# Who issues the stores of the scan-input stage: SyncE's queue or GpSimd's

## The chip, the cores and the metric

The kernel runs on one core of a Trainium2 chip. The metric is device time in microseconds (us) of one execution. TensorE (PE) multiplies matrices, VectorE (DVE) and ScalarE (ACT) work element by element, GpSimd (POOL) does so too, and SyncE (SP) here only issues DMAs. POOL can issue DMAs as well. An engine carries out its own instructions in the order in which they are written; semaphores order the engines among each other.

## The reference, cut to what matters

The program is a chain of four image networks; each is cut into stages that hand tensors over through memory. The change lies in the first stage of the last network, which prepares a selective scan:

```
xn = layernorm over the channels of x3, times ln_w, plus ln_b
xc, z = split(in_proj_w @ xn)                        # 192 channels each
xc = silu(depthwise 3x3 convolution(xc) + conv_b)
dts, B, C = split(x_proj_w @ xc)                     # 12 + 4 + 4 rows for each of 4 directions
z is needed later only as silu(z)
```

The stage writes `xc`, `zs` (silu of z), `dts` and `bcs` (B and C, each number split into three bf16 parts).

## The kernel before

`scan_inputs` works on 14 chunks, s = 0 to 13. A chunk is 8 image rows (448 columns) of two images together: 384 channels, laid as three tiles of 128 partitions. Each engine's program is one loop over s = 0 to 18 (`LAST`), and each loop step holds work of several chunks:

- PE in step s: `centre(s)` (the mean is taken off, from `xin`, line 2907 and the following, into `pA`), `project(s-1, 0)` (into `pI`, the half that becomes xc), `moment(s)` (the mean square, again line 2907 and the following), `small(s-4)` (lines 2951 to 2960: dts and B, C), `project(s-1, 1)` (the gate half).
- ACT in step s: `square(s)` (copies the centred chunk and squares it, lines 2985 and 2986), `maps(s-1)` and `halo(s-1)` (the convolution's input), `root(s)` (logarithm L3009 and exponential L3011), `small(s-4)`, `middle(s-4)`, a table load, `gates(s-1)` (silu of z into `zo`, L3031), `inputs(s-3)` (silu of the convolution into `xo`, L3037), a table load.
- DVE in step s: `taps(s-3, 0, 6)`, `normal(s)` (L3107, the normalised chunk `xn`), `remainder(s-4)`, `taps(s-3, 6, 9)`, `low(s-4)`. A tap is three instructions.
- SP in step s: the load of `xin` for chunk s (L2862; four buffers, so it needs `centred` of chunk s-4, `centred >= s-3`), then the store of `zo` of chunk s-1 (L2866), then for chunk s-4 the stores of `xo` (L2871), of `do` (two, L2874) and of `bo` (two, L2878). Each store stands behind the wait for what it stores:

```python
if live(s - 1):
    k = s - 1
    sp.wait_ge(z_evac, 3 * (k + 1))
    sp.dma_start(paired(zs)[k // NCH, :, :, span(k)], ...)
```

- POOL clears a few tiles at the start of the stage and has nothing more to do in it.

`zo`, `xo`, `do` and `bo` have three buffers each (`NO = 3`): `gates(s)` waits until the store of `zo` of chunk s-3 has landed, `inputs(s)` and `small(s)` until the five stores of chunk s-3 have. `centre(s)` waits for its load and for the logarithm of chunk s-1; `moment(s)` waits for the squares; `project(s, 0)` waits for `normal(s)`. A stage ends when all its stores have landed; the next one starts behind a barrier.

Of the kernel before, what the change touches and what calls it, by code (L numbers as in the profile page):

```python
# [18 lines left out]
NCH = 7  # L19
# [973 lines left out]
def paired(ap):  # L993

    return ap.rearrange("(q t p) n -> q p t n", t=3, p=128)
# [1759 lines left out]
def scan_inputs(nc, x3, ln_w, ln_b, in_wT, conv_w, conv_b, dts_wT, bc_wT, ident, xc, zs, dts, bcs):  # L2755
# [4 lines left out]
    with ExitStack() as ctx:  # L2760
# [3 lines left out]
        NX = 4  # L2764
        NO = 3
        NK = KD * RANK
# [15 lines left out]
        xin = [sb(f"f_xin{i}", [128, 3, CH]) for i in range(NX)]  # L2782
# [7 lines left out]
        xo = [sb(f"f_xo{i}", [128, 3, CH]) for i in range(NO)]  # L2790
        zo = [sb(f"f_zo{i}", [128, 3, CH]) for i in range(NO)]
        do = [sb(f"f_do{i}", [128, CH]) for i in range(NO)]
        rest = sb("f_rest", [64, CH])
        bo = [sb(f"f_bo{i}", [64, 3, CH], BF16) for i in range(NO)]
        pA, pI, pD, pB = pt("f_pa", 3), pt("f_pi", 3), pt("f_pd"), pt("f_pb")
        par_loaded = sem("f_par_loaded")
        in_loaded = [sem(f"f_in_loaded{i}") for i in range(NX)]
# [7 lines left out]
        centred = sem("f_centred")  # L2805
# [8 lines left out]
        z_evac = sem("f_z_evac")  # L2814
# [3 lines left out]
        silu_done = sem("f_silu_done")  # L2818
        dts_done = sem("f_dts_done")
        bc_done = sem("f_bc_done")  # L2820
        dts_evac = sem("f_dts_evac")
        hi_done = sem("f_hi_done")
        rest_done = sem("f_rest_done")
        mid_done = sem("f_mid_done")
        lo_done = sem("f_lo_done")
        z_stored = [sem(f"f_z_stored{i}") for i in range(NO)]
        x_stored = [sem(f"f_x_stored{i}") for i in range(NO)]
        block = ctx.enter_context(nc.Block())
        NS2 = 2 * NCH
        LAST = NS2 + 4  # L2830
# [6 lines left out]
        def live(s):  # L2837

            return 0 <= s < NS2

        def span(s):

            c = s % NCH
            return slice(c * CH, (c + 1) * CH)

        @block.sync
        def _(sp):
            sp.dma_start(xin[0][:, :, :], paired(x3)[0, :, :, span(0)]).then_inc(in_loaded[0], 16)
            sp.dma_start(idf[:, :], ident).then_inc(par_loaded, 16)
            sp.dma_start(w[:, :, :], in_wT.rearrange("(t p) o -> p t o", p=128)).then_inc(par_loaded, 16)  # L2850
            with nc.allow_non_contiguous_dma(reason="small vectors, once"):
                for dst, vec in ((cb, conv_b), (lg, ln_w), (lb, ln_b)):
                    sp.dma_start(dst[:, :], vec.rearrange("(t p) -> p t", p=128)).then_inc(par_loaded, 16)
                sp.dma_start(cw[:, :, :], conv_w.rearrange("(t p) k -> p t k", p=128)).then_inc(par_loaded, 16)
                sp.wait_ge(wide_set, 1)
                sp.dma_start(wt[:, :, 0:NK], dts_wT.rearrange("(t p) o -> p t o", p=128)).then_inc(par_loaded, 16)
                sp.dma_start(wb[:, :, :], bc_wT.rearrange("(t p) o -> p t o", p=128)).then_inc(par_loaded, 16)
            for s in range(LAST + 1):
                if live(s) and s:
                    if s >= NX:  # L2860
                        sp.wait_ge(centred, s - NX + 1)
                    sp.dma_start(xin[s % NX][:, :, :], paired(x3)[s // NCH, :, :, span(s)]).then_inc(in_loaded[s % NX], 16)  # L2862
                if live(s - 1):
                    k = s - 1
                    sp.wait_ge(z_evac, 3 * (k + 1))
                    sp.dma_start(paired(zs)[k // NCH, :, :, span(k)], zo[k % NO][:, :, :]).then_inc(z_stored[k % NO], 16)  # L2866
                if live(s - 4):
                    k = s - 4
                    q, o = k // NCH, k % NO
                    sp.wait_ge(silu_done, k + 1)  # L2870
                    sp.dma_start(paired(xc)[q, :, :, span(k)], xo[o][:, :, :]).then_inc(x_stored[o], 16)  # L2871
                    sp.wait_ge(dts_evac, k + 1)
                    for i in range(2):
                        sp.dma_start(dts[2 * q + i, :, span(k)], do[o][64 * i:64 * i + NK, :]).then_inc(x_stored[o], 16)  # L2874
                    sp.wait_ge(lo_done, k + 1)
                    sp.wait_ge(mid_done, k + 1)
                    for i in range(2):
                        sp.dma_start(bcs[2 * q + i, :, span(k)].rearrange("(m r) n -> r m n", m=3),  # L2878
                                     bo[o][32 * i:32 * i + 32, :, :]).then_inc(x_stored[o], 16)
            for o in range(NO):  # L2880
                n = len(range(o, NS2, NO))
                sp.wait_ge(z_stored[o], 16 * n)
                sp.wait_ge(x_stored[o], 80 * n)

        @block.gpsimd
        def _(p):
            p.memset(wt[:, :, :], 0.0).then_inc(wide_set, 1)
            p.memset(zero[:, :, :], 0.0).then_inc(cleared, 1)
            for i in range(4):
                p.memset(ct[i][:, :, :, :], 0.0).then_inc(cleared, 1)  # L2890

        @block.tensor
        def _(pe):
# [815 lines left out]
def network(nc, a, s, out):  # L3709

    batchnorm_qkv(nc, a["x"], a["bn_gamma"], a["bn_beta"], a["qkv1_wT"], a["qkv1_b"], s["qkvp"])
    window_attention(nc, s["qkvp"], a["dm_wT"], a["dm_b"], a["rel_bias"], a["tap_sel"], a["tap_block"], a["ident"], s["att"])
    mixer(nc, a["x"], s["att"], a["proj1_wT"], a["proj1_b"], a["c1_wT"], a["c1_b"], a["c2_wT"], a["c2_b"], s["x1p"], s["xp"])
    channel_gate(nc, s["x1p"], s["xp"], a["wg1T"], a["bn2"], a["wg2T"], a["bg2"], a["beta"], a["w1T"], a["bn1"],
                 a["basis"], a["chan"], a["ident"], s["gate"])
    window_inputs(nc, s["x1p"], s["gate"], a["n1g"], a["n1b"], a["qkv2_wT"], a["qk2_b"], a["qkv2_b"], a["temp"], a["tempr"],
                  a["ident"], s["qd"], s["kd"], s["vd"])
    window_strips(nc, s["qd"], s["kd"], s["vd"], a["biasT"], a["proj2_wT"], a["proj2_b"], a["ident"], s["pout"])
    detail_filter(nc, s["x1p"], s["gate"], s["pout"], a["hft_w"], a["hft_b"], a["ident"], s["x1"])
    forward_block(nc, s["x1"], a["n2g"], a["n2b"], a["fc1_wT"], a["fc1_b"], a["sgn_g"], a["sgn_b"], a["sg_w"], a["sg_b"],  # L3720
                  a["fc2_wT"], a["fc2_b"], a["ident"], s["x3"])
    scan_inputs(nc, s["x3"], a["ln_w"], a["ln_b"], a["in_wT"], a["conv_w"], a["conv_b"], a["dts_wT"], a["bc_wT"], a["ident"],
                s["xc"], s["zs"], s["dts"], s["bcs"])
    scans(nc, s["xc"], s["dts"], s["bcs"], a["dt_wT"], a["dt_b"], a["a_log"], a["ds"], a["bc_sel"], a["ident"], s["ys"])
    scan_outputs(nc, s["x3"], s["ys"], s["zs"], a["on_w"], a["on_b"], a["out_wT"], out)
# [55 lines left out]
```

## Time and profile before

| | |
|---|---|
| median of 3 runs | 6451.13 us (6445.07 to 6453.80) |
| the profiled execution | 6451.84 us, of which the profile spans 6450.2 us |
| the stage of the change | about 4289 to 4791 us of the span |

Times in the profile are us from the start of its span. Every sum of the prediction is made against the profiled execution's own 6451.84 us, and then set beside the median.

### The profile page before, as it was taken

How to read it: one execution, taken by the hardware profiler on the slowest of the kernel's cores; microseconds unless marked ns; L12 is line 12 of the kernel's file. 1: busy time of each engine (PE TensorE's matmuls, PEld its weight loads, DVE VectorE, ACT ScalarE, POOL GpSimd, SP SyncE). 2: the span in 40 equal slices, each digit the busy share in tenths (PEclk: the TensorE clock that was granted, in tenths of full speed). 3: DMA queues.
4: the chain of work that ended last, by engine and by line, in shares of the span. 5: the costliest groups of instructions: out<-in, count | busy, mean ns of one | idle time of the engine just before them, and what ended most of it. 6: DMA issues, size and time to landing. Idle time of an engine off the chain costs nothing. (4 is left out here: it accounts for less than half of the span.)

```text
span 6450.2 us, 87431 instructions
## 1 busy us (share of the span) xinstructions
PE 5460.1 (85%) x34828; PEld 2503.1 (39%) x34828; DVE 4288.2 (66%) x5132; ACT 2744.8 (43%) x3903; POOL 789.4 (12%) x814
## 2 busy tenths in 40 slices
PE   6959999999969978978878999967658888888867
PEld 2435455454434433445534344422213333333323
DVE  3267777777721112268877577755559999999978
ACT  1213333333332212235521544424448777777733
POOL 0000000000000001122243000000013333333300
PEclk9989999999979988999989999988779999999999
DMA  5431121121121114344433000011220000000035
GB/s 148 127 66 21 37 39 20 37 39 20 20 61 60 67 47 142 115 145 135 135 122 121 9 26 26 22 39 62 75 78 16 26 26 13 25 25 6 15 101 150
DMA packets 315553, 397.66 MB, mean 62 GB/s; under 512 B 160300, under 2 KB 297076, under 8 KB 311900
## 3 DMA queue, kind: packets, MB, share of 16 engines
q1 hardware_dynamic: 298396, 314.16, 17.8%
q0 software_dynamic: 16768, 78.09, 3.5%
q8 instruction: 271, 4.44, 0.3%
q14 instruction: 118, 0.97, 0.1%
HBM read 225.68 MB, written 166.50 MB: 61 GB/s over the span
## 5 line engine op out<-in xcount | busy, mean ns | idle before, releaser
L3643 DVE TENSOR_TENSOR_SCAN s_h<-s_da,s_h 128x448 f32<-128x448 f32 x672 | 733.2, 1135 | 1.1 <-ACT s_da L3570 1.0
L3490 PE MATMUL s_py<-s_prod,s_idf 128*128 128x448 f32 x1344 | 587.8, 560 | 23.5 <-ACT s_ycol L3583 22.3
L504 PE MATMUL b_pc<-b_ca,b_wdm 128*113 128x392 f32 x1152 | 485.3, 518 | 57.0 <-DVE b_idb L877 55.6
L3570 ACT ACTIVATE s_da<-s_dt,s_al 128x448 f32<-128x448 f32 x672 | 405.6, 657 | 199.2 <-DVE s_h L3643 149.0
L636 ACT ACTIVATE b_band<-b_psel 124x784 f32<-124x784 f32 x192 | 158.3, 824 | 602.8 <-PE b_psel L561 602.8
L504 PE MATMUL b_pc<-b_cb,b_wdm 128*113 128x392 f32 x960 | 409.5, 527 | 0.0
L3628 DVE TENSOR_TENSOR s_h<-s_dtu,s_pb 128x896 f32<-128x896 f32 x336 | 358.5, 1067 | 30.7 <-POOL s_dtu L3677 23.9
L3666 POOL TENSOR_TENSOR s_dt<-s_dt,s_dtu 128x448 f32<-128x448 f32 x168 | 249.5, 1485 | 951.4 <-ACT s_dtu L3560 526.0
L3650 DVE TENSOR_TENSOR s_prod<-s_h,s_pc 128x896 f32<-128x896 f32 x336 | 364.3, 1084 | 0.1
L929 DVE TENSOR_SCALAR b_band<-b_psel 124x784 f32<-124x784 f32 x192 | 186.8, 973 | 263.4 <-PE b_psel L561 261.2
L3490 PEld LDWEIGHTS s_py<-s_prod,s_idf 128*128 128x128 f32 x1344 | 250.2, 194 | 219.4 <-issue 167.9
L2699 DVE SCALAR_TENSOR_TENSOR j_zc<-j_zt,j_gw,j_zc 128x896 f32<-128x896 f32 x336 | 307.9, 990 | 0.0
L295 PE MATMUL a_ps<-a_x,a_wf 96*96 x672 | 259.6, 549 | 4.9 <-ACT a_out L270 4.9
L1171 ACT ACTIVATE c_hid<-c_ph,c_b 128x448 f32<-128x448 f32 x168 | 106.2, 634 | 332.1 <-PE c_ph L1132 318.4
L504 PEld LDWEIGHTS b_pc<-b_ca,b_wdm 128*113 128x113 f32 x1152 | 175.0, 177 | 160.2 <-issue 136.5
L1069 POOL MEMSET c_zero<- 128x1116 f32 x1 | 1.0, 1038 | 1875.3 <-POOLq L142 1875.3
L2226 PE MATMUL e_pc<-e_at,e_diag 128*128 128x448 f32 x504 | 192.5, 542 | 40.1 <-ACT e_at L2255 40.1
L620 ACT ACTIVATE b_at<-b_pbt 128x448 bf16<-128x448 bf16 x336 | 164.6, 543 | 129.1 <-PE b_pbt L546 129.1
L578 PE MATMUL b_po<-b_band,b_vt 124*32 124x112 f32 x5376 | 204.9, 277 | 1.6 <-issue 1.6
L3550 ACT ACTIVATE s_dt<-s_pd,s_db 128x448 f32<-128x448 f32 x168 | 144.0, 857 | 138.7 <-PE s_pd L3461 138.6
L3101 DVE SCALAR_TENSOR_TENSOR f_cv<-f_ct,f_cw,f_cv 128x448 f32<-128x448 f32 x336 | 202.3, 672 | 0.0
L578 PEld LDWEIGHTS b_po<-b_band,b_vt 124*32 124x32 f32 x5376 | 155.0, 112 | 104.2 <-issue 103.6
(624 smaller groups left out, 11328.0 us busy)
## 6 DMA issues: line engine op xcount, KB each, us to landing
mid_qkvp<-a_out SPq DMA_DIRECT2D x84, 372.0 KB, 4.0
b_qk<-mid_qkvp SPq DMA_DIRECT2D x96, 240.2 KB
d_vt<-mid_vd SPq DMA_DIRECT2D x200, 96.0 KB
d_qs<-mid_qd SPq DMA_DIRECT2D x20, 744.0 KB, 5.8
d_ks<-mid_kd SPq DMA_DIRECT2D x20, 744.0 KB, 7.9
b_v<-mid_qkvp SPq DMA_DIRECT2D x6, 1922.0 KB
mid_pout<-d_out POOLq DMA_DIRECT2D x20, 558.0 KB, 4.6
mid_x1p<-c_out POOLq DMA_DIRECT2D x14, 744.0 KB, 4.0
```

The lines of the kernel that those rows point to most:

```text
L295: last = pe.matmul(ps[n % 4][:, 0:CH], wf[:, g, m * G:(m + 1) * G], xs[:, g, b, c * CH:(c + 1) * CH], start=(g == 0), stop=(g == 1))
L504: mm = pe.matmul(pc[n % 2][0:113, 0:392], wdm[:, slot, p, 0:113], src, start=(w == STARTS[a]), stop=(w + 1 == STARTS[a + 1]))
L578: mm = pe.matmul(pO[32 * g:32 * g + 32, 112 * s:112 * s + 112], vt[:, 14 * hf + 4 * s + g + d, 32 * (h % 4):32 * (h % 4) + 32], band[hf][: ...
L2226: mm = pe.matmul(pc[k % 2][t][:, 0:CH], diag[:, t, i, :], at[k % 4][:, t, dy:dy + 8, dx:dx + W], start=(i == 0), stop=(i == 8))
L2699: v.scalar_tensor_tensor(dst, src, gw[:, t, k:k + 1], dst, ALU.mult, ALU.add).then_inc(tap_done, 1)
L3101: v.scalar_tensor_tensor(dst, tap, cw[:, t, k:k + 1], dst, ALU.mult, ALU.add).then_inc(tap_done, 1)
L3490: mm = pe.matmul(y, idf[:, :], prod[j % 3][:, e, :], start=(pr == 0 and e == 0), stop=False)
L3570: last = a.activation(da[j % 4][:, e, :], dt[s % 2][:, span(c)], ACT.Exp, scale=al[:, u, n:n + 1])
L3628: v.tensor_tensor(h[j % 4][:, :, :], u, pB[:, :, 0:CH], ALU.mult).then_inc(b_used, 1)
L3643: v.tensor_tensor_scan(x, along(da[j % 4][:, e, :]), x, before_, ALU.mult, ALU.add).then_inc(scanned, 1)
L3650: v.tensor_tensor(prod[j % 3][:, :, :], h[j % 4][:, :, :], pC[:, :, 0:CH], ALU.mult).then_inc(c_used, 1)
L3666: p.tensor_tensor(put(dt[s % 2]), put(dt[s % 2]), put(dtu[s % 2]), ALU.add).then_inc(dt_ready, 1)
```

## The change

All stores of the stage move from SP's program to POOL's. SP keeps the loads alone, each behind the wait for its buffer. On POOL a step s first stores the small outputs of chunk s-4, then the gate of chunk s-1, then the convolved input of chunk s-3 (before: of chunk s-4). What is stored, its size and its waits stay as they are. The waits for the end of all stores stay on SP.

```diff
-            for s in range(LAST + 1):
-                if live(s) and s:
-                    if s >= NX:
-                        sp.wait_ge(centred, s - NX + 1)
-                    sp.dma_start(xin[s % NX][:, :, :], paired(x3)[s // NCH, :, :, span(s)]).then_inc(in_loaded[s % NX], 16)
-                if live(s - 1):
-                    k = s - 1
-                    sp.wait_ge(z_evac, 3 * (k + 1))
-                    sp.dma_start(paired(zs)[k // NCH, :, :, span(k)], zo[k % NO][:, :, :]).then_inc(z_stored[k % NO], 16)
-                if live(s - 4):
...
+            for s in range(1, NS2):
+                if s >= NX:
+                    sp.wait_ge(centred, s - NX + 1)
+                sp.dma_start(xin[s % NX][:, :, :], paired(x3)[s // NCH, :, :, span(s)]).then_inc(in_loaded[s % NX], 16)
...
+            def store_gate(s):
+                p.wait_ge(z_evac, 3 * (s + 1))
+                p.dma_start(paired(zs)[s // NCH, :, :, span(s)], zo[s % NO][:, :, :]).then_inc(z_stored[s % NO], 16)
+            def store_input(s):
+                p.wait_ge(silu_done, s + 1)
+                p.dma_start(paired(xc)[s // NCH, :, :, span(s)], xo[s % NO][:, :, :]).then_inc(x_stored[s % NO], 16)
+            def store_small(s):
+                q, o = s // NCH, s % NO
+                p.wait_ge(dts_evac, s + 1)
+                for i in range(2):
+                    p.dma_start(dts[2 * q + i, :, span(s)], do[o][64 * i:64 * i + NK, :]).then_inc(x_stored[o], 16)
+                p.wait_ge(lo_done, s + 1)
+                p.wait_ge(mid_done, s + 1)
+                for i in range(2):
+                    p.dma_start(bcs[2 * q + i, :, span(s)].rearrange("(m r) n -> r m n", m=3),
+                                bo[o][32 * i:32 * i + 32, :, :]).then_inc(x_stored[o], 16)
+            for s in range(LAST + 1):
+                if live(s - 4):
+                    store_small(s - 4)
+                if live(s - 1):
+                    store_gate(s - 1)
+                if live(s - 3):
+                    store_input(s - 3)
```

## Rows read from the trace of the kernel before

**Rows 1.** Waits of the engines in the stage: total us, times, longest.
```profile
DVE f_xn L3107 <- ACT f_rs L3011: 220.0, 14, 24.3
...
PE f_pa L2907 <- DMA f_xin<-mid_x: 121.3, 12, 11.5
```

**Rows 2.** Timeline of PE at full rate early in the stage: start, duration.
```profile
4319.42 0.99 PE L2907 MATMUL f_pa<-f_xin,f_keep 128*128 128x448 f32 x2 [1.48 <-ACT f_rs L3009]
...
4323.70 1.02 PE L2936 MATMUL f_pi<-f_xn,f_w 128*128 128x448 f32 x2
```

**Rows 3.** Timeline of PE over one later step, from a centring to the next.
```profile
4499.25 1.86 PE L2907 MATMUL f_pa<-f_xin,f_keep 128*128 128x448 f32 x2 [11.35 <-DMA f_xin<-mid_x]
...
4505.80 1.02 PE L2936 MATMUL f_pi<-f_xn,f_w 128*128 128x448 f32 x2
...
4510.11 1.02 PE L2907 MATMUL f_pa<-f_sq,f_m 128*128 128x448 f32 x2
...
4514.32 0.54 PE L2951 MATMUL f_pd<-f_xo,f_wt 128*64 128x448 f32 x1
...
4517.82 1.02 PE L2936 MATMUL f_pi<-f_xn,f_w 128*128 128x448 f32 x2
...
4533.71 1.86 PE L2907 MATMUL f_pa<-f_xin,f_keep 128*128 128x448 f32 x2 [11.52 <-DMA f_xin<-mid_x]
```

**Rows 4.** Timeline of SP's queue over the same step.
```profile
4523.11 0.40 SPq L2866 DMA_DIRECT2D mid_zs<-f_zo  x1
...
4524.08 2.32 SPq L2874 DMA_DIRECT2D mid_dts<-f_do  x2
4526.50 1.95 SPq L2878 DMA_DIRECT2D mid_bcs<-f_bo  x2
4528.49 0.44 SPq L2862 DMA_DIRECT2D f_xin<-mid_x  x1
```

**Rows 5.** Windows: busy us (instructions) by engine, granted PE clock, DMA share, GB/s.
```profile
4505.80:4522.20 16.40, 16.39 (x60) 5.44 (x58) 4.99 (x8) 11.23 (x16) 0.00 (x0) 1.00 0.00 0
4414.48:4721.76 307.28, 207.23 (x650) 70.43 (x648) 163.70 (x270) 130.32 (x163) 0.00 (x0) 0.80 0.22 71
5080.00:5090.00 10.00, 8.63 (x41) 3.14 (x40) 10.00 (x11) 8.64 (x16) 2.92 (x4) 1.00 0.42 169
```

**Rows 6.** Timeline of DVE: the normalisations of chunks 1, 4 and 13.
```profile
4335.10 1.56 DVE L3107 TENSOR_TENSOR f_xn<-f_ce,f_rs 128x1344 f32<-128x1344 f32 x1 [12.88 <-ACT f_rs L3011]
...
4414.48 1.56 DVE L3107 TENSOR_TENSOR f_xn<-f_ce,f_rs 128x1344 f32<-128x1344 f32 x1 [9.85 <-ACT f_rs L3011]
...
4721.76 1.56 DVE L3107 TENSOR_TENSOR f_xn<-f_ce,f_rs 128x1344 f32<-128x1344 f32 x1 [16.15 <-ACT f_rs L3011]
```

**Rows 7.** Timeline of ACT over the same later step.
```profile
4505.92 1.29 ACT L2985 ACTIVATE f_ce<-f_pa 128x1344 f32<-128x1344 f32 x1 [12.83 <-PE f_pa L2913]
4507.11 1.28 ACT L2986 ACTIVATE f_sq<-f_pa 128x1344 f32<-128x1344 f32 x1
...
4514.53 1.29 ACT L3009 ACTIVATE f_rs<-f_pa 128x1344 f32<-128x1344 f32 x1 [2.61 <-PE f_pa L2913]
...
4524.75 1.32 ACT L3037 ACTIVATE f_xo<-f_cv 128x1344 f32<-128x1344 f32 x1 [1.67 <-DVE f_cv L3101]
4526.09 1.28 ACT L3057 ACT_TABLE_LOAD   x1
```

**Rows 8.** Stores that POOL issues in other stages: ns min/median/max.
```profile
L1556 POOL DMA_DIRECT2D mid_qd<-q_qo x14: 772/772/782, 2479.6 to 2770.3; - x14
...
L3681 POOL DMA_DIRECT2D mid_ys<-s_yrow x6: 571/584/597, 5084.1 to 6202.1; - x6
```

**Rows 9.** DMA issues of the page: KB each, median us to landing.
```profile
mid_kd<-q_ko POOLq DMA_DIRECT2D x14, 744.0 KB, 4.0
...
mid_xc<-f_xo SPq DMA_DIRECT2D x14, 672.0 KB, 4.8
```

**Rows 10.** The page's costliest groups: count | busy us, mean ns | idle before.
```profile
L3101 DVE SCALAR_TENSOR_TENSOR f_cv<-f_ct,f_cw,f_cv 128x448 f32<-128x448 f32 x336 | 202.3, 672 | 0.0
```

More of the change, by code:

```diff
@@ L2857, in _ @@
                 sp.dma_start(wb[:, :, :], bc_wT.rearrange("(t p) o -> p t o", p=128)).then_inc(par_loaded, 16)
-            for s in range(LAST + 1):
-                if live(s) and s:
-                    if s >= NX:
-                        sp.wait_ge(centred, s - NX + 1)
-                    sp.dma_start(xin[s % NX][:, :, :], paired(x3)[s // NCH, :, :, span(s)]).then_inc(in_loaded[s % NX], 16)
-                if live(s - 1):
-                    k = s - 1
-                    sp.wait_ge(z_evac, 3 * (k + 1))
-                    sp.dma_start(paired(zs)[k // NCH, :, :, span(k)], zo[k % NO][:, :, :]).then_inc(z_stored[k % NO], 16)
-                if live(s - 4):
[L2868 to L2879, printed above, removed]
+            for s in range(1, NS2):
+                if s >= NX:
+                    sp.wait_ge(centred, s - NX + 1)
+                sp.dma_start(xin[s % NX][:, :, :], paired(x3)[s // NCH, :, :, span(s)]).then_inc(in_loaded[s % NX], 16)
             for o in range(NO):
```

## The prediction

> **What bounds the kernel now.** The stage is a thirteenth of the span, so only what happens between 4289 and 4791 us counts. I read the waits of that stretch first. The largest is VectorE's, 220 us in front of the normalisation, and the root behind it is ScalarE's chain; but TensorE's own largest wait is 121.3 us, 12 times in 14 chunks, for the load of the chunk that it centres [rows 1]. Which of these is the cause is seen in the timelines of one step, with three engines side by side. TensorE finishes its five pieces at 4522.2 and stands until 4533.71, when the load lands [rows 3]. SyncE's queue shows why the load is late: it was issued at 4528.49, though the four buffers had long been free, because it stands behind the gate store, which waits for ScalarE's gates until 4523.11, and behind the issuing of that store and five more [rows 4]. So no load is ever ahead: each is issued after the work of the step before it is done. The idle 11.5 us are 0.9 us until the gates are ready, 5.4 us of issuing the six stores, and 5.2 us of load (4528.49 to 4533.71) [rows 3, 4]. There is a second price: after the pause the centring takes 6.55 us (4499.25 to 4505.80) where the same piece took 4.28 us without one (4319.42 to 4323.70) [rows 2, 3]; the granted clock is 0.80 over the nine steady steps and 1.00 in the busy part of one, the two levels being 1.2 and 2.4 GHz [rows 5]. Neither VectorE nor ScalarE bounds the steps: over nine of them they are busy 163.7 and 130.3 us, 18.2 and 14.5 a step, of 34.14 [rows 5, 6].
>
> **The change, part by part.**
>
> *Loads freed.* Loads 1 to 3 are issued at once, and load s as soon as chunk s-4 is centred, some three steps before its use; at 5.2 us a load it is hidden behind any step of over 2 us. The wait of 11.5 us and the slow first matmuls go.
>
> *What is late next, TensorE.* Its step without a pause is a sum of start-to-start times: project 4.31 (4505.80 to 4510.11), moment 4.21 (to 4514.32), small 3.50 (to 4517.82), the second project 4.31 like the first, and centring at the full clock 4.28 [rows 2, 3]. That is 20.6 us.
>
> *What is late next, the other loop.* From the logarithm of one chunk to that of the next there is also a way round through the other engines, since ScalarE can square chunk s+1 only after its own earlier work of step s: logarithm at 4514.53, silu of the convolution at 4524.75 (it waits for VectorE's last taps), end of the table load at 4527.37, then copy and squares 2.47 us (4505.92 to 4508.39), then moment until the next logarithm 4.42 us (4510.11 to 4514.53). 12.84 + 2.47 + 4.42 = 19.7 us [rows 3, 7]. This is 0.9 us under TensorE's step. VectorE's own 18.2 us is under both. So a steady step becomes 20.6 us, bounded by TensorE.
>
> *The stretch before the steady steps.* From the normalisation of chunk 1 to that of chunk 4 the kernel takes 79.4 us for three steps [rows 6]. `small` is not yet in them, so TensorE needs 20.6 - 3.5 = 17.1 us; for the third one ScalarE already has the silu of the convolution, and the 19.7 us loop decides. 17.1 + 17.1 + 19.7 = 53.9: a gain of 25.5 us. From chunk 4 to chunk 13 nine steps take 307.28 us, 34.14 each [rows 6]; they become 9 x 20.6 = 185.4, a gain of 121.9 us. Chunk 0 to 1 stays as it is: load 1 was issued early already. After the normalisation of chunk 13 nothing more is loaded and VectorE's taps run without a pause; those last 69 us stay.
>
> *Stores on GpSimd.* Six a step. The traces have no such store of the small outputs from GpSimd; of larger ones the issue takes 0.57 to 0.78 us [rows 8], and the small ones cost SyncE 1.0 to 1.2 each in the queue [rows 4]. Six are thus 3.5 to 7 us; I take 4.6 us (0.77 each), on an engine that is idle in this stage [rows 5]. Landing takes as long as from SyncE: 4.0 us for 744 KB against 4.8 for 672 KB [rows 9]. What could be queued behind a store on GpSimd is only the next store. In a step the small outputs of chunk s-4 are ready last, behind VectorE's last taps, so some 11 us after the logarithm [rows 7], and hold back the gate store by about 3 us and its six issues by 7 at most. The buffers are needed again by `inputs` two steps later, about 40 us after that, so a store that lands 5 us after its issue is over 25 us early. If that cover were gone each us of lateness would be a us of step. Cost in the steps: nothing.
>
> *At the end.* The last two stores start the end of the stage: two issues at 0.6 to 0.8 instead of 0.4, and perhaps a later landing. Lower bound 0, upper bound two issues of 1.2 and one more landing of 4.8 us that nothing covers, about 6; I take 1 us, since large stores land alike from both queues.
>
> Sum: 25.5 + 121.9 - 1 = 146.4 us. 6451.84 - 146.4 = 6305.4 us, and the median of the runs lies 0.7 us under the profiled execution, so 6305 us.
>
> **A rule weighed against the trace.** The scan stage shows GpSimd issuing a store at 5084.1 in 0.57 to 0.60 us, in a stretch in which VectorE is busy 10.00 of 10.00 us [rows 5, 8]: VectorE's work did not hold up descriptors there. The Trainium skill warns of the opposite (SBUF — State Buffer, section "SBUF: two separate sides"): a DMA from GpSimd's queue needs descriptors that GpSimd writes, and a VectorE instruction in a two-port mode locks it out of the port pair that both share, so that the DMA seems blocked. By the rows the sum is unchanged; by the rule it would be that of the last rival below.
>
> **The rivals.** (a) *The forecast*: 20.6 us steps, bounded by TensorE. Its own range: handovers that take up the 0.9 us between the two loops and lengthen steps by up to 1.3 us give 12 us more, and a gain at the start of the stage or no cost at the end a few less: 6296 to 6318. (b) *VectorE is held up while GpSimd issues.* If the two share a way to the memory, VectorE gets the 3.5 to 4.6 us of six issues on top of its 18.2: a step of 21.7 to 22.8, over TensorE's 20.6 by 1.1 to 2.2. Nine steps cost 10 to 20 us, and the four steps of the tail, where VectorE has no slack at all, 14 to 18 more: 6329 to 6343 (with the upper bound of 7 us for the six it would be 4.6 us on nine steps and 7 on four, 6374; I give that little weight, since no row of GpSimd is so dear). For it: VectorE's taps run back to back, so any loan shows. Against it: the scan stage with VectorE full has GpSimd work beside it all the time. (c) *The loop through ScalarE and VectorE is longer than I read*, because something that was long done in the slow steps comes last in the fast ones: 2 to 3 us a step, 12 steps, 6329 to 6341. (d) *Nothing changes*: the load is held by its own buffer, not by the queue. Then 6451. Against it: the buffer of the load at 4528.49 was read by the centring of four steps earlier, over 100 us before [rows 4, 6]. (e) *Slower*: the stores on GpSimd are held up by VectorE so long that output buffers are not free. Were each of the six held for one unbroken run of VectorE's work (16.6 us, its 18.2 a step less the normalisation of 1.56), a step would need 6 x 16.6 = 100 us, and ten steps at 66 us more than the 34.1 of now make about 7110 us. It decides from the point at which a store costs more than 34.14 / 6 = 5.7 us of GpSimd's time; the dearest row of GpSimd is 0.78 us [rows 8].
>
> **How the numbers follow.** Chances: (a) 0.74, (b) 0.12, (c) 0.10, (d) 0.02, (e) 0.02. The prediction is (a), 6305 us. The range has to leave out no more than 0.2; (a) and most of (b) and (c) lie between 6294 and 6340 us, and the far cases (d) and (e) stay outside. 0.2% of the time is 13 us, about what a measurement of this kernel can tell from no change; (a), (b) and (c) are all faster by far more. So faster 0.96, same 0.02, slower 0.02.
>
> **What would show it.** In the profile after: SyncE's loads of the stage issued one after the other behind centrings, TensorE's wait for the load gone from the list of waits, the granted clock near 1.00 in the steady steps, and normalisations 20.6 us apart from chunk 4 on. A step of exactly VectorE's busy time, or taps over their 672 ns [rows 10], would speak for (b). A new wait in front of `moment` for the squares, or of the squares for the table load, would speak for (c). Waits of `gates`, `small` or `inputs` for stores would speak for (e). The prediction is wrong if TensorE pauses for anything else in a steady step.

## The result

The changed kernel takes 6308.65 us (median of 4 runs, 6306.86 to 6310.96) against 6451.27 us before: a ratio of 0.9781, 95% interval 0.9764 to 0.9797. The forecast was 6305 us in a range of 6294 to 6340. A later repetition of the changed kernel gave 6308.24 us (5 runs, ratio 0.9778, 0.9761 to 0.9794). The profiled execution spans 6309.3 us, 140.9 us less than before.

Waits of the engines of the changed kernel between 4280 and 4700 us (total us, times, longest):
```profile
DVE f_xn L3118 <- ACT f_rs L3022: 74.4, 14, 16.3
ACT f_rs L3020 <- PE f_pa L2924: 42.8, 14, 5.9
```
The normalisation's wait, 220 us in [rows 1], is 74.4; TensorE's wait for `f_xin`, 121.3 us there, is not in the list at all. The queue of SyncE in the changed kernel shows why:
```profile
4294.61 188.18 SPq L2861 DMA_DIRECT2D f_xin<-mid_x  x13
4653.19 0.33 SPq L3416 DMA_DIRECT2D s_wd<-in_dt_wT  x1
```
Thirteen loads and nothing between them; the last is issued by 4482.8, 78 us before its chunk is centred. (The loads of [rows 4] stood each behind six stores.) One later step of TensorE in the timeline of the changed kernel, from a centring on:
```profile
4560.52 1.02 PE L2918 MATMUL f_pa<-f_xin,f_keep 128*128 128x448 f32 x2
4564.83 1.02 PE L2947 MATMUL f_pi<-f_xn,f_w 128*128 128x448 f32 x2
4569.13 1.02 PE L2918 MATMUL f_pa<-f_sq,f_m 128*128 128x448 f32 x2
4573.34 0.54 PE L2962 MATMUL f_pd<-f_xo,f_wt 128*64 128x448 f32 x1
4576.84 1.02 PE L2947 MATMUL f_pi<-f_xn,f_w 128*128 128x448 f32 x2
```
No idle time stands in front of any of them, and the centring is 4.31 us long to the next piece where [rows 3] had 6.55. The window over the eight steps before it, columns as in [rows 5]:
```profile
4391.26:4556.29 165.03, 165.03 (x577) 55.92 (x577) 145.52 (x241) 115.82 (x144) 30.12 (x48) 1.00 0.32 105
```
TensorE is busy all of 165.03 us at a granted clock of 1.00 (the upper of the two levels), where it was busy 207.23 of 307.28 us at 0.80. GpSimd's issuing is 30.12 us in eight steps, 3.8 a step. VectorE's normalisations of chunks 1, 4 and 13, and its last subtraction of the stage:
```profile
4336.83 1.56 DVE L3118 TENSOR_TENSOR f_xn<-f_ce,f_rs 128x1344 f32<-128x1344 f32 x1 [12.89 <-ACT f_rs L3022]
...
4390.57 1.56 DVE L3118 TENSOR_TENSOR f_xn<-f_ce,f_rs 128x1344 f32<-128x1344 f32 x1 [2.15 <-ACT f_rs L3022]
...
4576.23 1.56 DVE L3118 TENSOR_TENSOR f_xn<-f_ce,f_rs 128x1344 f32<-128x1344 f32 x1 [2.44 <-ACT f_rs L3022]
...
4643.34 0.62 DVE L3129 TENSOR_TENSOR f_bo<-f_rest,f_bo 64x448 bf16<-64x448 f32 x1 [0.64 <-ACT f_bo L3035]
```
From chunk 1 to 4 are 53.74 us (79.38 before), from 4 to 13 are 185.66 (307.28 before), 20.63 a step. The end of the stage went the other way. The last subtraction, the last two stores and the first DMA of the next stage, before:
```profile
4787.56 0.62 DVE L3118 TENSOR_TENSOR f_bo<-f_rest,f_bo 64x448 bf16<-64x448 f32 x1 [0.64 <-ACT f_bo L3024]
4788.20 0.79 SPq L2878 DMA_DIRECT2D mid_bcs<-f_bo  x2
4791.68 0.31 SPq L3405 DMA_DIRECT2D s_wd<-in_dt_wT  x1
```
and the last two stores in the changed kernel, issued by GpSimd:
```profile
4644.25 1.10 POOL L2892 DMA_DIRECT2D mid_bcs<-f_bo  x2 [3.75 <-DVE f_bo L3129]
```
From the start of the subtraction to the next stage are 4.12 us before and 9.85 after (4643.34 to 4653.19).

The stage as a whole, from its first DMA to the next stage's first, took 503.02 us before (4288.66 to 4791.68) and 364.65 after (4288.54 to 4653.19): 138.4 of the 140.9 us.

### The profile page after: what moved, and what is told of

The parts are those of the page before. It is cut to its first block and busy times, and to the rows that moved or that the text cites. A ratio compares the mean times of both kernels' runs of the same rounds, so it can differ in the third digit from the quotient of the medians.

```text
span 6309.3 us, 87431 instructions
## 1 busy us (share of the span) xinstructions
PE 5441.3 (86%) x34828; PEld 2497.5 (40%) x34828; DVE 4290.7 (68%) x5132; ACT 2743.8 (43%) x3903; POOL 840.7 (13%) x898
## 3 DMA queue, kind: packets, MB, share of 16 engines
q1 hardware_dynamic: 282268, 290.07, 17.1%
## 5 line engine op out<-in xcount | busy, mean ns | idle before, releaser
L253 DVE TENSOR_SCALAR a_out<-a_ps,a_bias 96x448 f32<-96x448 f32 x84 | 57.0, 681 | 206.5 <-PE a_ps L295 187.7
```

## The experiments

Besides the totals, the runs are compared by pieces of the stage that their timelines show. "Step" is the mean distance of the normalisations of chunks 4 to 13, "end" runs from the start of VectorE's last subtraction to the next stage's first DMA, "stage" from its first DMA to the next stage's. The totals down to "changed, last small stores on SyncE" are medians of 4 or 5 runs; each kernel below that row, and so each total there, was run once. One run lies up to 19 us from the median of its kernel (below), so where totals are less than some 20 us apart the pieces decide and not the total.

| kernel | total us | step | end | stage |
|---|---|---|---|---|
| before | 6451.27 | 34.14 | 4.12 | 503.02 |
| changed | 6308.65 | 20.63 | 9.85 | 364.65 |
| changed, again | 6308.24 | 20.63 | 9.85 | 361.61 |
| stores on SyncE, loads ahead | 6302.68 | 20.63 | 4.12 | 356.78 |
| the same, again | 6307.82 | 20.63 | 4.13 | 356.59 |
| changed, last small stores on SyncE | 6295.97 | 20.63 | 3.98 | 355.41 |
| before, gate store alone moved | 6411.92 | 31.80 | 4.12 | 457.38 |
| before, gate store alone stays | 6418.79 | 29.70 | 8.71 | 468.75 |
| loads ahead, last two stores on GpSimd | 6305.85 | 20.63 | 4.79 | 357.33 |
| changed, shorter `small` | 6295.48 | 19.85 | 9.84 | 352.78 |
| changed, two input buffers | 6314.5 | 20.63 | 9.83 | 362.48 |
| loads ahead, gates and last two on GpSimd | 6315.69 | 20.63 | 5.28 | 357.77 |
| loads ahead, bcs on GpSimd | 6297.99 | 20.63 | 5.73 | 357.66 |

**Loads ahead, every store on SyncE.** The kernel before with only the order of SyncE's program changed (`load(s)` is the wait and the DMA of the lines taken out):
```diff
+            load(1)
             for s in range(LAST + 1):
-                if live(s) and s:
-                    if s >= NX:
-                        sp.wait_ge(centred, s - NX + 1)
-                    sp.dma_start(xin[s % NX][:, :, :], ...)
+                if live(s + 2):
+                    load(s + 2)
```


> All stores stay on SyncE as before; only the order in SyncE's program changes: the load of chunk s+2 stands ahead of the stores of step s. Theory (the gain is the order of the loads, and who issues the stores does not matter): steady steps of 20.6 us from chunk 4 to 13, no wait of TensorE for loads in them, and an end of the stage of about 4.1 us from the last subtraction on VectorE to the first DMA of the next stage, as before, where the changed kernel took 9.85. Total about 6303 us, 5 to 6 under the changed kernel. Rival (a queue that only loads is needed, since the six issues of 5.4 us a step still hold up loads): steps above 22 us and a total above 6325 us.

Measured: 6302.68 us (ratio 0.9775, 0.9759 to 0.9791), step 20.63, end 4.12. A step of SyncE's queue in that run:
```profile
4498.62 3.48 SPq L2878 DMA_DIRECT2D mid_dts<-f_do  x2
4502.20 0.86 SPq L2882 DMA_DIRECT2D mid_bcs<-f_bo  x2
4503.10 0.44 SPq L2861 DMA_DIRECT2D f_xin<-mid_x  x1
```
The load still stands behind stores, but it is for two chunks later. All of the gain is in the order; nothing of it needs GpSimd.

**The last small stores on SyncE.** The changed kernel; the four small stores of chunk 13 follow SyncE's loads, on a semaphore of their own:
```diff
+            s = NS2 - 1
+            sp.wait_ge(dts_evac, s + 1)
+            for i in range(2):
+                sp.dma_start(dts[2 * q + i, :, span(s)], ...).then_inc(last_stored, 16)
+            sp.wait_ge(lo_done, s + 1)
+            sp.wait_ge(mid_done, s + 1)
+            for i in range(2):
+                sp.dma_start(bcs[2 * q + i, :, span(s)]..., ...).then_inc(last_stored, 16)
...
-                if live(s - 4):
+                if live(s - 4) and s - 4 < NS2 - 1:
                     store_small(s - 4)
```


> As the changed kernel, but the four small stores of the last chunk are issued by SyncE. Theory (GpSimd reaches the barrier at the end of the stage some 5 to 6 us after the last store that it issued has landed; its last one is then the convolved input of chunk 13, 8 us before the end): the stretch from VectorE's last subtraction to the next stage's first DMA falls from 9.85 to 4 to 5 us, total about 6303 us. Rival (a barrier costs more whenever GpSimd has issued stores in the stage at all, whenever they landed): the stretch stays at 9 us or more, total about 6308 us. Steady steps 20.6 us in either case.

Measured: end 3.98 us, though GpSimd still issued 80 of the 84 stores. Its last one and the next stage, in the timelines of GpSimd and of SyncE's queue:
```profile
4626.46 0.77 POOL L2894 DMA_DIRECT2D mid_xc<-f_xo  x1
4637.07 0.31 SPq L3428 DMA_DIRECT2D s_wd<-in_dt_wT  x1
```
So the longer end is GpSimd's lateness after its last store and nothing that every stage with such stores must pay. The total, 6295.97 us, fell by more than this piece of 5.9 us. In the two profiles 3.4 us more lie in pieces of the stage that the edit does not touch, and the stage began 6.9 us earlier, after stages in which the kernels are the same (below).

**Only the gate store moved; only the gate store kept.** The kernel before, with one part of the change each:
```diff
 (gate alone)
-                if live(s - 1):
-                    k = s - 1
-                    sp.wait_ge(z_evac, 3 * (k + 1))
-                    sp.dma_start(paired(zs)[k // NCH, :, :, span(k)], ...)
...
+            for k in range(NS2):
+                p.wait_ge(z_evac, 3 * (k + 1))
+                p.dma_start(paired(zs)[k // NCH, :, :, span(k)], ...)
```
and the converse, with the block under `if live(s - 4)` moved to GpSimd word for word and the gate store left on SyncE.

> The kernel before with the gate store alone moved to GpSimd; SyncE keeps the five stores of chunk s-4 ahead of the next load. Theory (the load comes after the last wait that stands before it): chunks 1 to 4 run without a pause as in the changed kernel, a gain of about 25 us; in the steady steps the load then waits for VectorE's last subtraction of chunk s-4 and the two stores behind it, at about 26.5 where it was 28.5, so steps of 32 us instead of 34.1 and about 18 us more. Total about 6407 us. Rival (the gate's wait, the longest in SyncE's queue by far, is what holds the loads): steps near 20.6 us and a total near 6305 us.

> The kernel before with the five stores of chunk s-4 moved to GpSimd; SyncE keeps the gate store ahead of the next load. Theory: chunks 1 to 4 as in the kernel before (79 us for three steps); in the steady steps the load is issued right after the gate store, 5 us earlier than before, so steps of about 29.1 us and 45 us gained; the end of the stage 5.7 us longer as in the changed kernel. Total about 6412 us. Together with the run that moves the gate alone the gains add up to some 85 us, not to the 143 of both: each wait hides the other. Rival (it is the issuing of stores that costs, so that four fifths of the gain lie in these five): a total under 6350 us.

Measured: 6411.92 and 6418.79 us. With the gate moved the steps are 31.80 us. A load now stands behind the small stores, and those behind VectorE's last subtraction (most of this queue's waiting is for `f_do`, the rest of it mainly for this one):
```profile
4524.40 0.80 SPq L2870 DMA_DIRECT2D mid_dts<-f_do  x2
4531.98 0.81 SPq L2874 DMA_DIRECT2D mid_bcs<-f_bo  x2
4532.83 0.44 SPq L2862 DMA_DIRECT2D f_xin<-mid_x  x1
```
With the gate kept they are 29.70 us, the load right behind it, and TensorE idle for it each time, from the timelines of SyncE's queue and of TensorE:
```profile
4512.62 0.38 SPq L2866 DMA_DIRECT2D mid_zs<-f_zo  x1
4513.05 0.49 SPq L2862 DMA_DIRECT2D f_xin<-mid_x  x1
...
4518.47 1.86 PE L2908 MATMUL f_pa<-f_xin,f_keep 128*128 128x448 f32 x2 [6.76 <-DMA f_xin<-mid_x]
```
The stage is 45.6 us shorter in the one and 34.3 in the other, 80 together, where the whole change gives 138. Each of the two waits hides behind the other; both rivals fall. (Both kernels were run once, but they differ from the others by far more than runs of one kernel do.)

**Shorter `small`.** The changed kernel without the matmuls of `small` over the middle tile (so dts, B and C lack its channels): 
```diff
-                pe.matmul(pD[lo, 0, 0:CH], wt[:, 0, :], x[:, 0, :], start=True, stop=False)
-                pe.matmul(pD[hi, 0, 0:CH], wt[:, 2, :], x[:, 2, :], start=True, stop=False)
-                pe.matmul(pD[lo, 0, 0:CH], wt[lo, 1, :], x[lo, 1, :], start=False, stop=True)
-                pe.matmul(pD[hi, 0, 0:CH], wt[hi, 1, :], x[hi, 1, :], start=False, stop=True).then_inc(dts_done, 1)
+                pe.matmul(pD[lo, 0, 0:CH], wt[:, 0, :], x[:, 0, :], start=True, stop=True)
+                pe.matmul(pD[hi, 0, 0:CH], wt[:, 2, :], x[:, 2, :], start=True, stop=True).then_inc(dts_done, 1)
...
```
and the same for `pB`.

> The changed kernel with half of the matmuls of small left out (those over the middle tile, so dts, B and C lack the channels of that tile): 1.77 us a step less on TensorE, 18.9 us. Theory (the loop through the logarithm, VectorE's last taps, silu, table load, squares and moment, 19.7 us, is next): steady steps of 19.7 to 19.8 us, TensorE idle before moment, total about 6300 us. Rival (TensorE alone sets the step and the loop was read too long): steps of 18.9 us and about 6293 us. If handovers add to the loop: over 20 us.

Measured: steps of 19.85 us. TensorE now waits in front of `moment` in its timeline, and ScalarE's timeline shows the loop:
```profile
4456.94 0.99 PE L2918 MATMUL f_pa<-f_sq,f_m 128*128 128x448 f32 x2 [0.97 <-ACT f_sq L2993]
```
```profile
4441.47 1.29 ACT L3016 ACTIVATE f_rs<-f_pa 128x1344 f32<-128x1344 f32 x1 [2.11 <-PE f_pa L2924]
...
4451.69 1.32 ACT L3044 ACTIVATE f_xo<-f_cv 128x1344 f32<-128x1344 f32 x1 [1.85 <-DVE f_cv L3108]
4453.03 1.28 ACT L3064 ACT_TABLE_LOAD   x1
4454.32 1.29 ACT L2992 ACTIVATE f_ce<-f_pa 128x1344 f32<-128x1344 f32 x1
4455.51 1.28 ACT L2993 ACTIVATE f_sq<-f_pa 128x1344 f32<-128x1344 f32 x1
...
4461.34 1.29 ACT L3016 ACTIVATE f_rs<-f_pa 128x1344 f32<-128x1344 f32 x1 [2.58 <-PE f_pa L2924]
```
From logarithm to logarithm are 19.87 us, squares right behind the table load. The forecast's 19.7 us was read from a slow step; the loop is there and 0.8 us under TensorE's step, not 0.9. The rival's 18.9 us falls.

**Two input buffers.** The changed kernel with `NX = 2` for `NX = 4`.

> The changed kernel with two input buffers instead of four, so that a load is issued one step before its use and no more. Theory (a load of 5.2 us needs to be ahead by less than one step of 20.6): steady steps of 20.6 us as in the changed kernel, total 6305 to 6312 us. Rival (four buffers are needed to have the gain): TensorE waits for loads again, steps over 21 us.

Measured: step 20.63 us, and no wait for `f_xin` in the list. The total of its one run, 6314.5 us, lies above the 6312 foreseen, but the stage took 362.48 us, between the two profiles of the changed kernel (364.65 and 361.61), and began 6.9 us later (4295.41) than in the first of them. One chunk of lead is enough here; the other two buffers buy nothing.

**What GpSimd does after its last store.** Three kernels with the loads ahead and the stores on SyncE, but for a few: the last two of bcs on GpSimd; those and the 14 gates; all 28 of bcs (with a semaphore of their own for each buffer). The first one's edit, the others are alike:
```diff
-                    for i in range(2):
+                    for i in range(2 if k < NS2 - 1 else 0):
                         sp.dma_start(bcs[2 * q + i, :, span(k)]..., ...)
...
+            p.wait_ge(lo_done, k + 1)
+            p.wait_ge(mid_done, k + 1)
+            for i in range(2):
+                p.dma_start(bcs[2 * q + i, :, span(k)]..., ...).then_inc(last_stored, 16)
```


> As the kernel with the loads ahead on SyncE and all stores on SyncE, but the last two of the stage's stores (bcs of chunk 13) are issued by GpSimd, its only DMAs of the stage. Theory (what counts is how late GpSimd's last store is, not how many it issued): the stretch from VectorE's last subtraction to the next stage's first DMA goes from 4.12 to 9 or 10 us. Rival (GpSimd has a backlog of all its stores to clear at the end of the stage): the stretch stays under 6 us. Total about 6308 us or 6303 us; the stretch decides, not the total.

> Loads ahead on SyncE; GpSimd issues the 14 gate stores and the last two of bcs, 16 in all with 14 x 384 + 2 x 96 = 5568 rows of memory, on 4 semaphores. Measured is the time from the end of GpSimd's last issue to the next stage's first DMA: 7.84 us with 84 issues (14784 rows, 6 semaphores), 6.69 us with 70 (9408 rows, 3 semaphores), 2.70 us with 2 (192 rows, 1 semaphore). Theory count (some 0.063 us for each DMA that GpSimd issued): 3.6 us. Theory rows (0.00035 us for each row): 4.6 us. Theory semaphores (each one that GpSimd's DMAs count on costs over 1 us): about 7 us.

> Loads ahead on SyncE; GpSimd issues the 28 stores of bcs, 28 x 96 = 2688 rows, on 3 semaphores of their own. Same measure. Theory count: 4.3 us, more than with the gates. Theory rows: 3.6 us, less than with the gates. Theory semaphores: about 6.7 us. Steady steps 20.6 us in all.

Measured, from the end of GpSimd's last issue to the next stage: 2.70 us with 2 stores, 3.25 with 16, 3.74 with 28, 6.69 with 70 (the kernel that keeps the gate), 7.84 with 84 (the changed kernel, 4645.35 to 4653.19, and again 7.84 in its repetition). With two stores only, in the timelines of GpSimd and of SyncE's queue:
```profile
4643.56 1.17 POOL L2902 DMA_DIRECT2D mid_bcs<-f_bo  x2 [347.05 <-DVE f_bo L3131]
4647.43 0.32 SPq L3418 DMA_DIRECT2D s_wd<-in_dt_wT  x1
```
The first of the three expectations named the wrong theory: the end is 4.79 us and not 9 or 10, so a late last store alone costs 0.7 us, and the other 5 us come with the stores that GpSimd issued earlier. The 2.70 us are in fact no lateness: after SyncE's own last two stores the kernel before takes 2.69 (4788.99 to 4791.68). The wait between the engines that ends the stage (L2760 in the waits of SyncE's queue) is 0.2 us in the kernel before and with 2 stores, 0.6 with 16, 0.5 with 28, 3.9 with 70 and 5.1 with 84. The profile puts it down to TensorE's queue; that GpSimd is the one that is late follows from the runs, since it comes and goes with GpSimd's stores alone.

The order of the five values is that of the number of stores. The semaphores (7 us foreseen with 4 or 3 of them) and the rows written (which would put 28 small stores below 16 mostly large ones) don't give it. A straight line does not either: the count theory foresaw 3.6 and 4.3. Nor is the number shown to be the cause. In these kernels the stores also stand the closer together the more there are: none, one, two, five and six a step. An earlier stage of the kernel before speaks against either as the only cause. It has 68 stores from GpSimd (12 at its start, then four in about 22.7 us), and its last issue and the first DMA behind it are:
```profile
2780.15 1.33 POOL L1561 DMA_DIRECT2D mid_vd<-q_vo  x2 [1.84 <-DVE q_vo L1745]
2787.03 0.36 SPq L1830 DMA_DIRECT2D d_qs<-mid_qd  x1
```
That is 5.55 us, the landing of the last stores included, with a wait between the engines of 0.5 us, where 70 stores here, five in a step of 29.70 us, leave 6.69 us and a wait of 3.9. What sets the amount stays open. What GpSimd does in that time the profile does not show; it is idle there in every view.

**The two versions side by side.**

> The changed kernel once more, beside the next one on the same chip: about 6309 us.

> The kernel with the loads ahead and all stores on SyncE once more. Theory (who issues the stores changes only the end of the stage, by 5.7 us): 5 to 6 us under the changed kernel, steady steps of 20.6 us in both. Rival (the difference of the two medians so far, 6 us, is what stages elsewhere in the program happened to take): no difference between the medians.

Measured, five runs each beside each other: 6308.24 us (6289.28 to 6313.69) and 6307.82 us (6299.10 to 6313.77). The stage is 5.0 us shorter with the stores on SyncE (356.59 against 361.61), but in these two profiles it also began 5.0 us later (4291.37 against 4286.33), after stages in which the kernels are the same. Runs of one kernel spread by up to 24 us here, so 5 us, under 0.1%, are shown in the stage and not in the total. For the same reason the 6295.97 us of the kernel with the last small stores on SyncE is no proof of a better total: its stage began 6.9 us earlier than the changed kernel's. No version was found whose total is shown to beat the changed kernel.

## Why the prediction was right, step by step

- **The cause.** That the load was late because of its place in SyncE's queue: shown, since reordering that queue alone gives the same steps of 20.63 us and the same total. Rival (d), that nothing changes, is out.
- **The TensorE step.** Forecast 20.6 us from start-to-start times of two stretches without a pause, measured 20.63. The slow matmuls after the pause went as said, granted clock 1.00.
- **The other loop.** Forecast 19.7 us, measured 19.85 once TensorE was made shorter. In the step from chunk 3 to 4, where it decides, it took 19.28 us (4371.29 to 4390.57), and not 19.7, since VectorE has no `remainder` (0.61 us) to do in it yet; the two steps before took 17.23 each for the forecast 17.1. The errors cancel: 53.74 against 53.9 us. Rival (c), a loop 2 to 3 us longer than read, is out.
- **VectorE beside GpSimd's issuing, rival (b).** In the page's group of taps of the changed kernel
```profile
L3112 DVE SCALAR_TENSOR_TENSOR f_cv<-f_ct,f_cw,f_cv 128x448 f32<-128x448 f32 x336 | 202.3, 671 | 0.0
```
  the mean is 671 ns where [rows 10] has 672, with 84 stores issued beside them. VectorE lent nothing, in the steps or in the tail.
- **GpSimd's issues.** Forecast 0.77 us each and bounds of 3.5 to 7 us for the six; a step takes 3.8. From the groups of the changed kernel (ns min/median/max):
```profile
L2877 POOL DMA_DIRECT2D mid_zs<-f_zo x14: 754/768/780, 4340.1 to 4602.4; - x14
L2882 POOL DMA_DIRECT2D mid_xc<-f_xo x14: 748/753/768, 4379.9 to 4635.5; - x14
L2888 POOL DMA_DIRECT2D mid_dts<-f_do x28: 514/529/540, 4391.3 to 4640.0; - x28
L2892 POOL DMA_DIRECT2D mid_bcs<-f_bo x28: 552/553/675, 4398.9 to 4644.8; - x28
```
  The upper bound came from the 1.0 to 1.2 us that a small store costs SyncE in [rows 4]. That is not the price of the store itself: with no store right ahead of it, a pair cost SyncE 0.78 us (4784.62) and 0.79 (4788.20) in the same kernel. No store was late for its buffer: no wait for one stands in the lists of `gates`, `small` or `inputs`. Rival (e), stores held up until output buffers are not free, is out: the dearest of the 84 issues took 780 ns, though VectorE was busy 145.52 of 165.03 us. What the rule of the Trainium skill ("SBUF — State Buffer", section "SBUF: two separate sides") would do did not show either; whether VectorE was ever in a two-port mode, no run here shows.
- **The end of the stage.** This term was mis-sized: 1 us taken, 0 to 6 as bounds, 5.7 measured (9.85 - 4.12). The prediction costed the issue and the landing of the last two stores, which together are 0.7 us (4.79 - 4.12), and missed the 5 us in which GpSimd, after 84 stores, holds up the next stage though the stores have landed. The waits of SyncE's queue in the changed kernel between 4630 and 4655 us (total us, times, longest) show it:
```profile
SPq L2865 <- DMA mid_bcs<-f_bo: 164.2, 1, 164.2
SPq L2760 <- PEq L2760: 5.1, 1, 5.1
```
  The wait for the stores, from its last load at 4482.8 on, is over at about 4647.0; 5.1 us more go in the wait between the engines that ends the stage, and the next one begins at 4653.19. That 5.7 us still lies within the bounds is luck: they were made from a dearer issue and a later landing, and neither came.
- **The sum.** In the first profile 3.2 us more came from pieces that the change does not touch: from the stage's first DMA to the first normalisation are 33.85 us (4288.54 to 4322.39) where the kernel before has 32.00 (4288.66 to 4320.66), and the tail from chunk 13 to the last subtraction is 67.11 us where it was 65.80. The repetition has 31.95 and 65.96 for the two, so neither belongs to the change. There the stage is 141.4 us shorter, which is the forecast's 147.4 us of its steps less 5.7 us of its end, to 0.3 us.

## What to carry to other kernels

A queue is an order: a load behind a store waits for what the store waits for. Before an engine is given the stores, try moving the load ahead of them; here that alone gave all of it. Where several waits stand in front of one thing, each half of the change gives much less than its share (45.6 and 34.3 of 138 us, 80 together), so a first try that brings little proves little. The new step can be read from the old trace, if the start-to-start times are taken from stretches without a pause, and if the second-longest way round is summed as well: here it is 0.8 us under the first, and would be the bound after the next 4% off TensorE.

## What had not been expected of the hardware

After GpSimd has issued many stores in this stage, the next stage begins later, though the stores have landed: 2.70, 3.25, 3.74, 6.69 and 7.84 us after the end of its last issue with 2, 16, 28, 70 and 84 stores, where 2.69 follow SyncE's own last store. What sets the amount is not shown: number and spacing grow together in these kernels, and 68 stores in another stage left 5.55 us, not some 6.6. The lateness is hidden when GpSimd's last store is early: 80 stores with the last issued some 10 us before the end of the stage (4626.46 against 4637.07) cost nothing.
